# A decoder layer with 160 routed experts: two short last pages share one entry, and the round goes from thirteen entries to ten

## The reference, cut to what matters

```
logits = x @ router_w.T + expert_bias            # 2048 x 160
top_w, top_idx = top_k(sigmoid(logits), 8)
top_w = 2.5 * top_w / (sum(top_w) + 1e-9)
h1 = silu(einsum('th,eih->eti', x, w_gate))      # 160 experts, 256 -> 128
routed = einsum('eti,ehi->th', h1 * combine, w_down)
shared = silu(x @ w_gate_shared.T) @ w_down_shared.T
```

## Time and profile before

| | |
|---|---|
| median of three runs | 947.88 us (942.7 to 948.03) |
| profiled execution | 945.26 us |
| its span | 943.40 us |
| mean granted TensorE clock over the span | 0.916 |
| busy: TensorE, VectorE, ScalarE, GpSimd | 83%, 54%, 44%, 39% |
| experts' stage, first transpose to the end of the last scatter | 590.25 to 885.03 us |
| combining stage | 885.03 to 943.40 us |

### The profile page before, as it was taken

The page is one execution under the profiler, slowest core; times in us unless marked ns, Lnnn a source line. Parts: engine busy times, 40 slices in busy tenths (PEclk is TensorE's granted clock), DMA queues, the critical chain, the costliest instruction groups (busy, mean ns, idle before and its releaser), DMA issues. The chain is left out here.

```text
span 943.4 us, 15828 instructions
## 1 busy us (share of the span) xinstructions
PE 781.7 (83%) x3874; PEld 513.5 (54%) x3874; DVE 507.4 (54%) x1297; ACT 414.6 (44%) x887; POOL 369.8 (39%) x367
## 2 busy tenths in 40 slices
PE   8999999999995897988889410999999799983295
PEld 4543333333333384755646310888888688772173
DVE  1677877877813237577582880444444343430087
ACT  2247767777772426153432100456555455441011
POOL 9000000000000000347477775477777677777400
PEclk9999999999997798899989755999999999997599
DMA  6899777778561011224132228899999999961495
GB/s 241 298 318 310 269 237 293 261 246 291 215 251 51 22 46 45 94 81 152 71 106 98 104 103 278 277 379 373 367 377 362 318 314 350 316 223 58 189 422 227
DMA packets 110272, 213.04 MB, mean 226 GB/s; under 512 B 27735, under 2 KB 58369, under 8 KB 103952
## 3 DMA queue, kind: packets, MB, share of 16 engines
q1 hardware_dynamic: 62240, 146.18, 44.4%
q0 software_dynamic: 16752, 35.20, 10.1%
q10 hardware_dynamic: 31232, 31.09, 9.7%
HBM read 123.35 MB, written 101.19 MB: 238 GB/s over the span
## 5 line engine op out<-in xcount | busy, mean ns | idle before, releaser
L1662 POOL DMA_INDIRECT contributions<-c_c,e_dest x221 | 215.7, 976 | 86.8 <-issue 55.2
L1810 POOL DMA_INDIRECT row_pool<-rows,places x128 | 131.6, 1028 | 160.0 <-issue 136.0
L518 DVE TENSOR_REDUCE a_mx<-a_psS 128x2 f32<-128x1024 f32 x128 | 152.0, 1218 | 32.8 <-PE a_psS L341 32.6
L1613 DVE COPY e_xt<-e_psx 128x256 f32<-128x256 f32 (+1 forms) x169 | 84.8, 506 | 151.9 <-PE e_psx L1551 142.6
L476 ACT ACTIVATE a_e<-a_psT 128x512 f32<-128x512 f32 x256 | 137.9, 596 | 54.7 <-PE a_psT L371 50.0
L1562 PE MATMUL e_psg<-e_xt,e_w 128*128 128x128 f32 (+1 forms) x676 | 131.3, 318 | 18.2 <-DVE e_xt L1613 8.1
L1571 PE MATMUL e_psy<-e_w,e_g 128*128 128x256 f32 x442 | 125.9, 387 | 0.0
L1636 ACT ACTIVATE e_g<-e_psg 128x128 f32<-128x128 f32 (+1 forms) x169 | 52.5, 310 | 162.6 <-PE e_psg L1562 128.1
L1643 ACT ACTIVATE c_c<-e_psy,e_weight 128x256 f32<-128x256 f32 x221 | 98.7, 472 | 35.9 <-PE e_psy L1571 23.4
L1562 PEld LDWEIGHTS e_psg<-e_xt,e_w 128*128 128x128 f32 x676 | 100.9, 198 | 23.7 <-issue 11.4
L762 POOL MEMSET m_ones<- 128x128 bf16 (+2 forms) x3 | 0.5, 219 | 267.4 <-POOLq L165 267.4
(11 more groups left out here) (261 smaller groups left out, 963.7 us busy)
## 6 DMA issues: line engine op xcount, KB each, us to landing
e_w<-w SPq DMA_DIRECT2D x169, 256.0 KB
row_pool<-fill SPq DMA_DIRECT2D x32, 1260.0 KB, 7.2
rows<-row_pool ACTq DMA_DIRECT2D x204, 140.0 KB
c_c<-contributions SPq DMA_DIRECT2D x16, 1024.0 KB, 17.4
a_k<-k_parts SPq DMA_DIRECT2D x64, 128.0 KB, 3.4
a_q<-q_parts SPq DMA_DIRECT2D x32, 128.0 KB, 3.9
a_q<-q_parts SPq DMA_DIRECT2D x64, 64.0 KB, 3.4
contributions<-c_c,e_dest POOLq DMA_INDIRECT x221
```

The source lines that it names most:

```text
L518: nc.vector.tensor_reduce(mx[:, at.slot, qt, 2 * DH * pair::HALF], psS[:, pair], AX, ALU.max).then_inc(maxed, 1)
L1613: nc.vector.tensor_copy(XT[:, at.slot % XT_RING, 0:n], ps_x(at, 0, n)).then_inc(xt_done, 1)
L1662: nc.gpsimd.indirect_dma_start(out=contrib, out_offset=bass.IndirectOffsetOnAxis(ap=dest[:, result(f) + k:result(f) + k + 1], axis=0), in_ ...
L1810: nc.gpsimd.indirect_dma_start(out=pool, out_offset=bass.IndirectOffsetOnAxis(ap=place[:, b, t, k:k + 1], axis=0), in_=rows[:, b, t], in_o ...
```

## The change

The odd pages are split into two kinds. A short is an odd last page of at most 64 rows, up to a limit of six ninths of the odd pages plus one; the rest stay single. Two shorts of different experts form a twin: their rows are loaded into partitions 0 to 63 and 64 to 127 of one place, are transposed together, get gate matmuls of 64 columns each with their own weights (four matmuls where a single has two), share one SiLU, get down matmuls into 64 partitions each, and share one weighted copy and one scatter. A round is ten entries, `"tpopt" + "opopt"`: four pairs, three twins and three singles, with fourteen pages, thirteen sets of weights and seventeen row loads. The rounds are counted in threes, 1 + 3 x `more`, in a loop of fixed length 18, and there are three rounds of result places.

```diff
-PAIRS, ONES = 4, 9
-PAIRED = (False, True, False, False, True, False, False, False, True, False, False, True, False)
-RING_E = PAIRS + ONES
-PAGES_E = 2 * PAIRS + ONES
+PAIRS, TWINS, ONES = 4, 3, 3
+SHORTS, SHORT = 2 * TWINS, P // 2
+KINDS = "tpopt" + "opopt"
+RING_E = PAIRS + TWINS + ONES
+WEIGHTS_E = PAIRS + SHORTS + ONES
+PAGES_E = 2 * PAIRS + TWINS + ONES
-ENTRIES_OF = (range(0, 7), range(7, RING_E))
+ENTRIES_OF = (range(0, 5), range(5, RING_E))
-BODIES = 33
+TURN = 3
+TURNS = 18
+BODIES = 1 + TURN * TURNS
...
-                    pe.wait_ge(shared_added, 1)
-                    for i in range(7):
+                    pe.wait_ge(shared_added, 2)
+                    for i in range(COLUMNS):
...
+                    do(nc.vector.tensor_tensor(shorts[:], pages_i[:], count[:], ALU.subtract))
...
+                    do(nc.vector.scalar_tensor_tensor(shorts[:], shorts[:], float(P - SHORT), odds[:], ALU.is_ge, ALU.mult))
+                    sync()
+                    do(nc.vector.tensor_tensor_scan(shorts_to[:], ones_row[:], shorts[:], 0.0, ALU.mult, ALU.add))
+                    do(nc.vector.tensor_scalar(short_limit[:], odds_to[:, EXPERTS - 1:], float(SHORTS) / (SHORTS + ONES), 1.0,
+                                               ALU.mult, ALU.add))
...
+                    do(nc.vector.scalar_tensor_tensor(shorts[:], shorts_to[:], short_limit[:], shorts[:], ALU.is_le, ALU.mult))
+                    sync()
+                    do(nc.vector.tensor_tensor_scan(shorts_to[:], ones_row[:], shorts[:], 0.0, ALU.mult, ALU.add))
+                    do(nc.vector.tensor_tensor(odds[:], odds[:], shorts[:], ALU.subtract))
+                    sync()
+                    do(nc.vector.tensor_tensor_scan(odds_to[:], ones_row[:], odds[:], 0.0, ALU.mult, ALU.add))
...
+        elif KINDS[slot] == "t":
+            for k in range(2):
+                number = pages[loads.start + k]
+                sp.dma_start(self.X[SHORT * k:SHORT * (k + 1), place], pool[bass.ds(number * P, SHORT)]).then_inc(here, 16)
...
-    RESULTS = 2
+    RESULTS = TURN
     AHEAD = RING_E - DOWN_LAG
...
-    XT_RING = 7
+    XT_RING = 5
...
-            with eng.Fori(0, (BODIES - 1) // 2) as i:
+            with eng.Fori(0, TURNS) as i:
                 with eng.If(i < more):
-                    for k in range(first, first + 2 * RING_E):
-                        step(At(i * 2, k, RING_E))
+                    for k in range(first, first + TURN * RING_E):
+                        step(At(i * TURN, k, RING_E))
...
-                    for c in range(DC):
-                        last = nc.tensor.matmul(ps_g(f, n), W[:, f.slot, c * INTER:(c + 1) * INTER],
-                                                XT[:, f.slot % XT_RING, c * n:(c + 1) * n], start=c == 0, stop=c == DC - 1)
+                    own = n // weights_of[f.slot]
+                    for k, place in enumerate(WEIGHTS_FOR[f.slot]):
+                        for c in range(DC):
+                            at0 = c * n + k * own
+                            last = nc.tensor.matmul(ps_g(f, n)[:, k * own:(k + 1) * own], W[:, place, c * INTER:(c + 1) * INTER],
+                                                    XT[:, f.slot % XT_RING, at0:at0 + own], start=c == 0, stop=c == DC - 1)
...
-                        last = nc.tensor.matmul(ps_y(f, k), G[:, f.slot % XT_RING, k * P:(k + 1) * P],
-                                                W[:, f.slot, DC * INTER:], start=True, stop=True)
+                        high = P // weights_of[f.slot]
+                        for i, place in enumerate(WEIGHTS_FOR[f.slot]):
+                            last = nc.tensor.matmul(ps_y(f, k)[i * high:(i + 1) * high],
+                                                    G[:, f.slot % XT_RING, k * P + i * high:k * P + (i + 1) * high],
+                                                    W[:, place, DC * INTER:], start=True, stop=True)
```

More of the change, by code:

```diff
@@ new lines @@
+HALVES = 2
+ENTRIES_OF = (range(0, 5), range(5, RING_E))
+PAIRS_IN, TWINS_IN, ONES_IN = (tuple(KINDS[own.start:own.stop].count(kind) for own in ENTRIES_OF) for kind in "pto")
+WEIGHTS_IN, PAGES_IN = (tuple(p * PAIRS_IN[h] + t * TWINS_IN[h] + ONES_IN[h] for h in range(HALVES)) for p, t in ((1, 2), (2, 1)))
+LOADS_IN = tuple(PAGES_IN[h] + TWINS_IN[h] for h in range(HALVES))
+WEIGHTS_OF, PAGES_OF = (tuple(slice(sum(own[:h]), sum(own[:h + 1])) for h in range(HALVES)) for own in (WEIGHTS_IN, PAGES_IN))
@@ L77, in first_page @@
[L77 to L83, removed]
+assert WEIGHTS_IN[0] <= EXPERTS_AT[1] and WEIGHTS_IN[1] <= PAGES_AT[0] - EXPERTS_AT[1] and max(LOADS_IN) <= 16
+TURN = 3
+TURNS = 18
+BODIES = 1 + TURN * TURNS
+COLUMNS = 9
+THIRDS, SIXTHS = 342, 171
+assert PAIRS == 4 and ONES == TURN == 3 and SHORTS == 6
+SHORT_BANK = 6
+HALF_OF = tuple(int(j >= ENTRIES_OF[1].start) for j in range(RING_E))
@@ new lines, in columns @@
+def columns(j, sizes):
+    h, kind = HALF_OF[j], KINDS[j]
+    before = {"p": 0, "t": sizes["p"] * PAIRS_IN[h], "o": sizes["p"] * PAIRS_IN[h] + sizes["t"] * TWINS_IN[h]}[kind]
+    first = before + sizes[kind] * KINDS[ENTRIES_OF[h].start:j].count(kind)
+    return range(first, first + sizes[kind])
+EXPERTS_FOR, PAGES_FOR, LOADS_FOR = (tuple(columns(j, dict(zip("pto", sizes))) for j in range(RING_E))
+                                     for sizes in ((1, 2, 1), (2, 1, 1), (2, 2, 1)))
+PLACE_OF = tuple(PAGES_OF[HALF_OF[j]].start + PAGES_FOR[j].start for j in range(RING_E))
@@ L84 @@
+WEIGHTS_FOR = tuple(range(WEIGHTS_OF[HALF_OF[j]].start + EXPERTS_FOR[j].start, WEIGHTS_OF[HALF_OF[j]].start + EXPERTS_FOR[j].stop)
+                    for j in range(RING_E))
 LN_EPS = 1e-5
@@ L749, in _ @@
             for j in range(RING_E):
[L750 removed]
+                tables.load_weights(sp, w, j, first[HALF_OF[j]])
             for r in range(2):
@@ L1315, in fill_tables @@
                                                        -1.0, float(EXPERTS), ALU.mult, ALU.add))
-                        do(nc.vector.tensor_scalar(tables.expert[:, 0:full, first + 2 * pairs_here:PAGES_OF[h].stop],
+                        twin_at = slice(first + 2 * pairs_here, first + 2 * pairs_here + twins_here)
+                        for i in range(2):
+                            where = slice(SHORT * i, SHORT * (i + 1))
+                            do(nc.vector.tensor_scalar(tables.expert[where, 0:shorts_full, twin_at],
+                                                       short(0)[where, :, shorts_own.start + i:shorts_own.stop:2],
+                                                       -1.0, float(EXPERTS), ALU.mult, ALU.add))
+                        do(nc.vector.tensor_scalar(tables.expert[:, 0:full, twin_at.stop:PAGES_OF[h].stop],
                                                    alone(0)[:, :, ones_to_here:ones_to_here + ones_here],
@@ L1457, in experts @@
     GATE_LAG, DOWN_LAG = 2, 4
-    RESULTS = 2
+    RESULTS = TURN
     AHEAD = RING_E - DOWN_LAG
-    pages_of = [1 + pair for pair in PAIRED]
+    pages_of, weights_of = [len(own) for own in PAGES_FOR], [len(own) for own in WEIGHTS_FOR]
+    loads_of = [len(own) for own in LOADS_FOR]
     pages_before = [sum(pages_of[:j]) for j in range(RING_E)]
     body = lambda at: at.i + at.k // RING_E
-    half = lambda at: int(at.slot >= ENTRIES_OF[1].start)
+    half = lambda at: HALF_OF[at.slot]
     at_half = lambda at: body(at) * HALVES + half(at)
@@ L1470, in experts @@
     pages_done = lambda at: body(at) * PAGES_E + pages_before[at.slot]
-    pages_in = [own.stop - own.start for own in PAGES_OF]
+    pages_in = PAGES_IN
     ALL = BODIES * RING_E
```

119 lines of the change are left out of this document (69 added, 50 removed).

## The result

Time after: 952.8 us median of ten runs (from 949.5), beside 945.9 for the kernel before (ten runs, 942.7 to 948.3). The ratio is 1.0084, 95% interval 1.0062 to 1.0106: 0.8% slower, where 907 us was predicted (896 to 924), 4% faster. Seven of the ten lie between 949.5 and 953.9, two at 958.6, and one single run took 1840 us, which no other run of this study repeats and the ratio leaves out. The profiled execution took 951.38 us, its span 949.6, at a mean granted clock of 0.906.

The account below looks back on a forecast made before the run. GpSimd's scatters were taken to bound the experts' stage; afterwards GpSimd, TensorE and DMA lie within 4%. The stage's end moves from 885.03 to 844.2, so 947.9 - 40.8 = 907 us, range 896 to 924 (forecast alone 896 to 914).

Parts of the forecast that it names:

- Is the round count kept: Experts' stage: the change keeps 13 rounds, with entries going from 169 to 130.
- GpSimd: Scatters of results in the experts' stage: 39 fewer at 1.281 us, 50.0 us off; alone it would end the stage at 831.9.
- TensorE: Matmuls of the experts' stage: a twin takes 1.55 to 1.95 us, a round 16.7 to 17.9.
- Larger code per pass (30 steps for 26) stalls the queues at each turn: Rival for the turns of the experts' loop: 4 x 2 us, 914 us; chance 4%.
- Other engines: ScalarE and VectorE in the experts' stage: both had slack, so their part costs nothing.
- The end of the loops: Skipped passes, 14 instead of 10, lose their cover: 14.7 us on TensorE before the last four entries.
- my sum: Experts' stage end: 592.44 plus 13 rounds of 17.5, less 2.9, plus 14.7, 11 and 1.5, giving 844.2 us.
- The start: Before the experts' stage: tables built near 8.7 us later, delaying the start 0 to 4 us, taken as 1.5.
- DMA: Experts' stage: 6.71 MB a round against a steady mean of 372 GB/s; 17.5 us taken as the round's pace.
- Half loads: Rival for twins' row loads: each costs DMA as much as a whole one, round near 18.6 us, 921; chance 18%.
- GpSimd waits for its own landings: Rival at half rounds of scatters: waits for the previous round's same half, 14 us, 920; chance 9%.

Follow-up runs that it names:

- the kernel with the short pass: The change with two rounds instead of three in a pass of the loop, 14 passes still skipped, two rounds of result places: 918.6 us, 0.9746 of the kernel before.
- half of the skips: The change with two rounds in a pass and its 27 passes in nine groups of three, 7 skips: 909.8 us, 0.9655 of the kernel before.
- picking later: Two rounds in a pass without skips, with VectorE's picking one entry later in each half: 0.9572 of the kernel before on a slower chip, 0.9567 without it.
- 227: The kernel before with one padding semaphore instruction after each step of ScalarE, 227 instructions a pass: 1036.3 us, 1.099 of the kernel before.
- 253: The kernel before with two padding semaphore increments after each step of ScalarE, 253 instructions a pass: 965.6 us, 1.0248 of the kernel before.
- 279: The kernel before with three padding semaphore increments after each step of ScalarE, 279 instructions a pass: 966.2 us, 1.0235 of the kernel before.

## Why the prediction was wrong

The last scatter was predicted to end at 844.2 us and ended at 891.4, 47 us later. By the prediction's steps:

- **Is the round count kept, and GpSimd.** Right: 13 rounds, 182 scatters, 974 ns each. GpSimd stopped being the bound, as forecast.
- **TensorE.** Right. Side by side is how the twin's down matmuls run, 0.58 us for four (0.43 to 0.55 was that end), the gate 0.84 (0.87 to 0.97); an undisturbed round takes 17.50 us, within the 16.7 to 17.9. TensorE works through all of it (busy 17.50 us of the 17.50 from 804.81), so this is its own pace. The twin by its parts would give 3 x 1.64 + 3 x 1.10 + 4 x 2.17 = 16.9; the groups beside a twin's down matmuls run 0.05 to 0.1 us longer (0.54 us from 746.25 for a gate that takes 0.44 from 751.36).
- **The rival "Larger code per pass (30 steps for 26) stalls the queues at each turn".** This is the failed step: the mechanism was named, given 4%, and priced at "4 x 2 us". It happened at three turns and cost 34.9 us, 11.6 each. The price took account of a queue standing for a moment, not of ScalarE standing twice (12 us in all), of TensorE standing for its results (22.3 us over the three turns), and of TensorE's clock falling after the stops (0.82, 0.83 and 0.77 in those rounds, 12.5 us). The reason for the low chance, no gap at the turns in the trace of before, says nothing about a longer pass: the change itself takes the condition away, by 264 instructions of ScalarE in a pass for 201.
- **Other engines, "I costed their part at nothing".** Wrong for ScalarE, and the same error seen from its side: it was 41% busy by the page, and its share of busy time doesn't count waits, semaphore and DMA instructions, of which its pass mostly consists.
- **The end of the loops.** Mechanism right, size short: 14.7 us on TensorE predicted, 11.54 + 8.76 = 20.3 measured. In the kernel with the short pass the same 14 skips cost 15.1, so the other 5.2 belong to the long pass. As a whole, with the clock at 0.61 to 0.77 from the first stop on, the stretch from the last round's first transpose to the last scatter took 53.5 us (837.86 to 891.38) against 40.2 in my sum (804.0 to 844.2). That the skips were on the path is shown by the kernel without them, 21 us faster.
- **The start.** 8.7 us later for the tables predicted, 7.05 measured; 1.5 for the start, 2.5 measured. The sum counts its rounds from 592.44, which is the edge of a window and not the start of a round: in the kernel before the first transpose is at 590.25 and the second round begins at 607.72, 3.4 us before the 611.11 of the sum. So the second round of the change began at 608.18 where my sum has 611.4, 3.3 us early.
- **DMA.** Overestimated a little, and the 17.5 was right by luck: it was taken as DMA's pace, DMA did not hold it, and the rounds of the change that do take 17.50 us have it from TensorE. Where nothing else stops, two rounds in a pass run at 18.3 us a round. In this kernel from 610 to 812 us DMA moved 73.72 MB at 365 GB/s, 6.67 MB in 18.3 us: the predicted bytes of 6.71 MB, at 2% less than the 372 of the earlier trace rows. Over the eleven rounds after the first that is 8.6 us more than the sum has. The change does not show it, its rounds between the stops run at 17.5.
- **Half loads** and **GpSimd waits for its own landings.** The first did not come: a half load counted as a whole one would make a round 7.14 MB, 19.2 us at the 372 GB/s of the earlier trace rows, and it takes 18.3. The packets say so too. From 645 to 812 us the row loads' queue took 36.4% of the 16 engines' time for 144 whole loads in the kernel before, and 33.3% for 100 whole and 56 half ones with two rounds in a pass: 0.25% for a whole load, 0.14% for a half. Of the second no wait worth a row shows: 0.6 us in total from 610 to 812.

The account against my sum, for the change's trace, counted between the first transposes of rounds: 35.7 for the turns (rounds of 29.15, 29.48 and 29.57 us), 1.5 for the eight others, 13.3 for the end, less 3.3 for the early second round, give 47. With the stops at the turns gone, the kernel of two rounds in a pass ends at 858.0, still 14 above my sum: 8.6 for eleven rounds at 18.3, 8.2 for the end, less 3.0 since its second round began at 608.42. Its 918.6 us lies inside the predicted range, at 2.5% below the kernel before where 4% was forecast. With half of the skips it ends at 847.0 and takes 909.8; this is close to 907, but it is no longer the kernel of the forecast, which had 14 skips in it. What was computed of the change was thus near, with errors of both signs; what was missed is its loop.

Open: why DMA gave 365 GB/s and 18.3 us a round though single rounds take 17.50. VectorE waited 62 us in 202 for rows there, but picking later gained nothing (on the slower chip). Open also: what makes a stop 5 to 7 us long. It is not shown to be competition with the row and weight loads: ScalarE's first stop in the change (653.6 to 660.1) lies under full traffic, 365 GB/s, and its second (660.7 to 666.2) is nearly as long at 67 GB/s. Open too: where exactly ScalarE's limit lies between 201 and 227 (234 and 260 compiled), whether it is a count of instructions or depends on where blocks of code lie, and why a skipped pass fetches code at 227 (8.7 us each) and hardly at 253, 264 or 279 (11.5, 14.6 and 11.4 us for all).

## What to carry to other kernels

When a change puts more steps into a pass of a loop, count the instructions of each engine in it as compiled, waits and DMA issues included, and ask what happens at the turn; the quiet turns of the shorter pass are no evidence. An engine on whose results others wait is priced by what stops behind it: 12 us of ScalarE standing cost 11.6 us of the whole core at each turn though ScalarE is busy 41% of the time. And when the bound is taken away, look at what it covered: of skipped passes that were taken to be free under GpSimd's backlog, 14 cost 21 us without it, and skipping them in groups brought 9 us back.

## What was not expected of the hardware

- ScalarE's loop of 201 instructions (234 compiled) turned without a stop, of 227 to 279 (260 to 314 compiled) with a stop of 4 to 8 us, mostly two, at each turn, in two different kernels; TensorE's of 263 (588 compiled) gave none in the kernel before. The packets of the queue q14 that come with the stops are 8 KB each.
- Where DMA is nearly idle (17 GB/s), five such packets come in 8.7 us, one every 1.7 us, though each keeps a DMA engine for 0.46 us.
- Four matmuls of 256 f32 columns into two separate halves of the partitions take 0.58 us, and 0.86 in line.
- A row load of 70 KB into half of the partitions kept the DMA engines busy for 0.14% of a stretch in which one of 140 KB into all of them took 0.25%.
- The kernel before took 943 to 946 us (medians) in three sets of runs and 1092 to 1094 in two, on other chips; on one of these DMA moved 241 GB/s (in its version without skips) for 349 from 650 to 800 us. Why is not known.
